# Casting the high halves of queries and keys on ScalarE instead of VectorE

## What is computed

```python
qkv = x_flat @ qkv_w.T + qkv_b
q, k, v = (qkv[0], qkv[1], qkv[2])
q = _l2norm(q)
k = _l2norm(k)
attn = jnp.einsum('bhnd,bhmd->bhnm', q, k) * temperature
attn = jax.nn.softmax(attn, axis=-1)
out = jnp.einsum('bhnm,bhmd->bhnd', attn, v)
```

## Time and profile before

| | us |
|---|---|
| median of 3 runs | 2742.59 (2740.02 to 2743.46) |
| the profiled execution | 2741.01 |
| its span, first to last instruction | 2739.1 |
| of that before the first exponential | 109.6 |
| attention, first to last exponential | 109.6 to 1652.0 |
| TensorE busy | 2465.8 (90%) |
| ScalarE busy | 1780.7 (65%) |
| VectorE busy | 1683.5 (61%) |
| GpSimd busy | 1420.5 (52%) |

### The profile page before, as it was taken

How to read it: one execution, slowest core, us unless ns; L and a number is a source line. 1 busy time by engine, 2 the same in 40 slices (tenths; PEclk the granted TensorE clock), 3 DMA queues, 4 the chain that set the end, 5 groups by cost and what they waited for, 6 DMA issues and landing times. The chain is left out here.

```text
span 2739.1 us, 58873 instructions
## 1 busy us (share of the span) xinstructions
PE 2465.8 (90%) x18693; PEld 1295.9 (47%) x18693; DVE 1683.5 (61%) x4886; ACT 1780.7 (65%) x2228; POOL 1420.5 (52%) x1137
## 2 busy tenths in 40 slices
PE   3699999999989999989999973999999999999975
PEld 2333333333333333333333321777777777777754
DVE  6557766866766766676676655555555555555522
ACT  2487777777778777767777852555565556555542
POOL 2334435534543543543454323677777777777750
PEclk9799999999999999999999987999999999999987
DMA  4221112112112111211211243444444444444429
GB/s 91 58 51 41 50 49 58 48 42 54 51 44 60 48 49 47 58 41 45 59 48 45 77 162 128 179 155 155 177 155 162 169 155 170 160 158 174 153 79 332
DMA packets 160322, 276.49 MB, mean 101 GB/s; under 512 B 21568, under 2 KB 129584, under 8 KB 150624
## 3 DMA queue, kind: packets, MB, share of 16 engines
q1 hardware_dynamic: 141648, 245.37, 27.8%
q0 software_dynamic: 13392, 27.97, 2.8%
q10 hardware_dynamic: 5056, 0.42, 0.3%
HBM read 174.07 MB, written 49.69 MB: 82 GB/s over the span
## 5 line engine op out<-in xcount | busy, mean ns | idle before, releaser
L788 ACT ACTIVATE probs<-ps_s 128x1024 f32<-128x1024 f32 x1024 | 1011.9, 1023 | 282.6 <-PE ps_s L687 260.0
L1360 POOL TENSOR_TENSOR h_split<-h_f,h_split 128x512 f16<-128x512 f32 x444 | 550.7, 1241 | 238.3 <-ACT h_f L1337 231.0
L1333 ACT ACTIVATE h_split<-ps_h,packs 128x512 f16<-128x512 f32 x444 | 305.2, 687 | 391.1 <-PE ps_h L1287 368.8
L1287 PE MATMUL ps_h<-m_xn_t,packs 128*128 128x512 f16 x2220 | 552.4, 380 | 0.5 <-DVE m_xn_t L1422 0.5
L700 PE MATMUL ps_o<-probs,v_aug 128*32 128x512 f32 x4096 | 550.6, 610 | 0.4 <-ACT probs L788 0.4
L1054 POOL TENSOR_TENSOR inv_norm<-sumsq,minus_half 128x16 f32<-128x16 f32 x128 | 378.0, 2953 | 312.4 <-DVE sumsq L997 307.6
L1301 PE MATMUL ps_y<-packs,h_split 128*128 128x192 f16 x5328 | 511.9, 245 | 0.9 <-POOL h_split L1360 0.9
L1301 PEld LDWEIGHTS ps_y<-packs,h_split 128*128 128x128 f16 x5328 | 453.0, 97 | 105.7 <-POOL h_split L1360 1.9
L687 PE MATMUL ps_s<-stacks_odd 98*128 98x512 f16 x1024 | 301.5, 386 | 17.0 <-DMA stacks_odd<-heads 10.2
L687 PE MATMUL ps_s<-even 98*128 98x512 f16 x1024 | 299.0, 383 | 11.6 <-ACT probs L788 5.7
L1337 ACT ACTIVATE h_f<-ps_h,packs 128x512 f32<-128x512 f32 x444 | 302.0, 680 | 0.0
(11 more groups left out here) (213 smaller groups left out, 2812.6 us busy)
## 6 DMA issues: line engine op xcount, KB each, us to landing
packs<-expert_pack SPq DMA_DIRECT2D x74, 1635.0 KB, 6.6
even<-heads SPq DMA_DIRECT2D x192, 96.0 KB, 2.4
stacks_odd<-heads SPq DMA_DIRECT2D x192, 96.0 KB, 2.4
tile_rows<-sorted_rows SPq DMA_DIRECT2D x37, 400.0 KB
tokens<-in_x_dram SPq DMA_DIRECT2D x17, 768.0 KB, 5.3
y_in<-y_tokens SPq DMA_DIRECT2D x16, 768.0 KB, 8.9
out_dram<-y_out SPq DMA_DIRECT2D x16, 768.0 KB, 7.1
even<-heads SPq DMA_DIRECT2D x128, 48.0 KB
```

What stands on the lines that cost most here:

```text
L788: act.activation(probs[:, u % PRING, :], ps_s[:, u % 2, :, :].rearrange("p f n -> p (f n)"), ACT.Exp).then_inc(s_probs, 1)
L1287: mm = pe.matmul(ps_h[:, n % HBUF, :], w1(par, slot, w, k), xn_t[0:rows_k, par, c, :], start=(i == 0), stop=(i == 4))
L1333: act.activation(h_split[:, n % HSPLIT, 0, :], ps_h[:, n % HBUF, :], ACT.Gelu, bias=bias1(par, slot, k), scale=1.0 / WSCALE)
L1360: pool.tensor_tensor(h_split[:, n % HSPLIT, 1, :], h_f32[:, n % HBUF, :], h_split[:, n % HSPLIT, 0, :], ALU.subtract).then_inc(s_h, 1)
```

## The change

ScalarE makes the high half of tile r-1, behind the exponential and the jobs of unit U+1 (`HIGH_AT = 1`). Two semaphores are new: `s_scaled` says that the scaling (L1007) has ended, and ScalarE waits for it; `s_high` says that the cast has ended, and VectorE waits for it ahead of the low half. VectorE's cast and its own wait behind it are gone. The low half stays in unit U+3.

```diff
+HIGH_AT = 1
-PRE_STEPS = 50 + NT
+PRE_STEPS = 50 - NT
...
+            if has_pre(img) and u - HIGH_AT in ROUNDS[1:NT + 1]:
+                high_heads(act, img, ROUNDS.index(u - HIGH_AT) - 1)
+
+    def high_heads(act, img, t):
+
+        act.wait_ge(s_scaled, NT * (img + 1) + t + 1)
+        if t >= QRING:
+            wait_taken(act, img, ("q", t - QRING))
+        elif not (isinstance(img, int) and img == -1):
+            act.wait_ge(s_job_act, jobs_before(img, True))
+        act.activation(qk_split[:, t % QRING, :, 0:HD], qk[:, t % QKRING, :, :], ACT.Copy).then_inc(s_high, 1)
...
-            pre.now(dve.tensor_tensor(qk[:, t % QKRING, :, :], scale16[:, :].unsqueeze(2).to_broadcast([P, 2 * NH, HD]),
-                                      qk[:, t % QKRING, :, :], ALU.mult))
-        elif part == 1:
-            if t >= QRING:
-                wait_taken(dve, img, ("q", t - QRING))
-            pre.now(dve.tensor_copy(high, qk[:, t % QKRING, :, :]))
+            dve.tensor_tensor(qk[:, t % QKRING, :, :], scale16[:, :].unsqueeze(2).to_broadcast([P, 2 * NH, HD]),
+                              qk[:, t % QKRING, :, :], ALU.mult).then_inc(s_scaled, 1)
+            dve.wait_ge(s_scaled, NT * (img + 1) + t + 1)
         else:
+            dve.wait_ge(s_high, NT * (img + 1) + t + 1)
             dve.tensor_tensor(low, qk[:, t % QKRING, :, :], high, ALU.subtract).then_inc(s_qk, 1)
...
-                if v in (0, 2, 3) and 0 < r <= NT:
-                    split_heads(dve, img, r - 1, pre, (0, 2, 3).index(v))
+                if v in (0, 3) and 0 < r <= NT:
+                    split_heads(dve, img, r - 1, pre, (0, 3).index(v))
```

More of the change, by code:

```diff
@@ L594, in attention_phase @@
     s_qk = sem("s_qk")
+    s_scaled = sem("s_scaled")
+    s_high = sem("s_high")
     s_rep_q, s_rep_k = ([sem(f"s_rep_{kind}{r}") for r in range(2)] for kind in "qk")
```

## The result

The changed kernel takes 2770.63 us as a median (2768.79 to 2771.19, 4 runs) against 2742.79 (2740.02 to 2743.46, 4 runs) for the kernel before beside it: a ratio of 1.0103, 95% interval 1.0091 to 1.0115. That is 27.8 us more, where +20 was predicted. The sign was right and 2770.6 lies inside the range, but about a third of the loss came from a place that the prediction didn't look at.

The account below looks back on a forecast made before the run. TensorE was taken to pace attention, so relief of VectorE gains nothing. Twelve loop images cost 14.9 us, images 1 and 2 2.4, image 0 3.7, less 0.5: 20.5 on 2741.0, about 2762 as a median, range 2739 to 2780.

Parts of the forecast that it names:

- What bounds the kernel: Attention phase: TensorE paces it; VectorE giving up 128 casts, 46 us of busy time, gains 0 there.
- ScalarE's step: Each cast lasts 512 ns on ScalarE and, as instructions overlap, delays what follows by about 0.42 us (bounds 0.39 and 0.51).
- Tiles 5, 6, 7 in the loop: Late exponentials delay TensorE's scores by 0.42, 0.06 and 0.76 us, the last by waiting for VectorE's scaling: 1.24 an image.
- Tiles 0 to 4 hidden: In an image of the loop, the casts of the first five tiles cost TensorE nothing.
- The sum: Whole kernel: 20.5 us added to the profiled 2741.0 gives 2761.5, about 2762 for a median, 0.7% slower.
- Image -1, "0.5 us gained": Before the first scores: only the last tile's cast is on the path, and moving it to ScalarE gains 0.5 us.
- Images 0 and 1: Image 0 loses 3.7 us: 0.42 each for tiles 1 to 6, 1.19 for tile 7; image 1 about 1.2.
- The rule weighed: VectorE's cast blocks GpSimd through a shared port; without it the power ends up to 0.36 earlier, 2758 us; left out.
- the waits of rows 2: TensorE's waits for VectorE's "v" eviction (L839): 33.5 us in 42 waits over 1544 us, forecast to stay near 33.
- full cost for every cast: Rival: no tile is hidden, 120 casts by 0.42 are 50 us, tile 7's wait adds 5: 2798; chance 0.08.
- the two with relief: Rivals: VectorE's relief offsets ScalarE's load, 2743, chance 0.16; or earlier "v" evictions gain 15 to 19 us, 2725, chance 0.12.
- What would show it: Signs: cast 0.49 to 0.53 us, ScalarE idle some 0.35 at tile 7, loop image 1.2 longer, expert phase unchanged.

Follow-up runs that it names:

- e8_five_pad20: Changed kernel with only tiles 0 to 4 cast on ScalarE, plus 20 unused VectorE writes so its loop starts at 740: 2733.44 us, ratio 0.9997.
- e12_last_three_pad12: Changed kernel with only tiles 5, 6, 7 cast on ScalarE, plus 12 unused VectorE writes (loop from 740): 2751.81 us, ratio 1.0079.
- e13_unit_two_pad32: Changed kernel with all eight casts one unit later, behind the jobs of unit U+2, plus 32 unused VectorE writes: 2747.50 us, ratio 1.0051.
- e4_first_five: Changed kernel with only tiles 0 to 4 cast on ScalarE, tiles 5 to 7 back on VectorE, no unused writes: 2750.52 us, ratio 1.0036.
- e3_no_cast: Kernel before without any cast: high halves zero, low half the whole number in f16, ScalarE as before: 2740.69 us, ratio 0.9995.

## Why the prediction was right, and where it fell short

- **What bounds the kernel**: right. TensorE paces it, and 46 us taken from VectorE bought nothing: 0.9995 (0.9984 to 1.0006) without any cast.
- **ScalarE's step**: 0.42 predicted, 0.41 measured; the cast 512 and 514 ns.
- **Tiles 5, 6, 7 in the loop**: 1.24 predicted, 1.16 measured where the code lies well, 1.17 as the mean of the change on the first chip, where the twelve bodies gave 14.1 against 14.9.
- **Tiles 0 to 4 hidden**: right in the loop (`e8_five_pad20`, `e12_last_three_pad12`). Wrong for image -1.
- **The sum**: 2761.5 for the profiled execution and 1.6 for the median give 2763, not "about 2762"; nothing hangs on it. That 2770.6 lies inside the range is luck in part. The prediction had no term for the returns; terms that were too large (image 0, the bodies) and the last image's 2.0 took back a part of what they cost.
- **Image -1, "0.5 us gained"**: half right. With only the last three tiles on ScalarE the first exponential comes at 108.81 instead of 109.44, 0.63 gained. In the change it comes 0.25 later, since the cast of tile 0 stands ahead of the third "n" eviction on ScalarE. That eviction was at 56.41 and is now at 58.94, behind the cast:

```profile
58.51 0.52 ACT L823 ACTIVATE heads<-heads 128x384 f16<-128x384 f32 x1 [4.85 <-DVE heads L1021]
58.94 0.47 ACT L802 ACTIVATE xn_t<-ps_m 128x384 f16<-128x384 f16 x1
```

  The step that failed is "image -1 has no exponentials ... the cast is no part of that": I asked what the cast delays, and not what stands behind its new wait. With the cast behind the "n" eviction (`e13_unit_two_pad32`) it is 108.73.
- **Images 0 and 1**: image 0 cost 2.8 instead of 3.7, image 1 3.5 instead of 1.2. At the end of image 0, TensorE waits 1.29 us for an exponential, and then works at the lower clock (0.50 from 189 to 191):

```profile
185.98 0.61 PE L690 MATMUL ps_s<-even 98*128 98x512 f16 x2 [1.29 <-ACT probs L791]
186.89 0.60 PE L690 MATMUL ps_s<-even 98*128 98x512 f16 x2 [0.31 <-ACT probs L791]
187.43 1.81 PE L703 MATMUL ps_o<-probs,v_aug 128*32 128x512 f32 x8
```

  The kernel before has no drop there. Over image 1 the other kernels with casts or copies at the last tiles lose between 1.4 and 3.9 us on either chip. Some 1.2 of it goes with the clock: the changed kernel on the second chip has no such fall, and image 1 takes 106.25 there instead of 107.43 (103.94 before). Of the 2.3 that are left, 1.2 was forecast; the rest stays open.
- **The missing term**: "the sum" knew only bodies. The step that failed is that the five jumps back to the loop's start were put at nothing, without a reason. VectorE's code became shorter by 32 instructions ahead of the loop and by 60 in it, and with that its restart became later, at least 4.47 us instead of 3.56, and TensorE waited up to 2.4 us for `tokens`. Five returns cost 9.9 us on the first chip, 7.6 on the second, the share of the clock in it included; small stalls of the same kind inside the iterations cost 0.6 an iteration there. On one chip the shift took back 10.6 us of the 33.7 that the change costs there (2766.64, 2755.99, 2732.98). That the cause is the place of VectorE's instructions is shown by the shifts. Which places are bad isn't: starts at 708 and 720 are, 740 and 772 aren't, and `e3_no_cast`, from 709 and with 122 transfers, isn't either. What the restart waits for stays open: more transfers of instructions go with the late restart of the change, but the times of single ones don't fit both late kernels.
- **The rule weighed**, of the Trainium skill (SBUF — State Buffer, "SBUF: two separate sides"): the trace spoke against it and the runs agree. Freed of the cast, the power takes 2917 ns for 2954 before, 0.04 shorter and not 0.36, and the waits of rows 2 grew from 33.5 to 38.4 instead of shrinking by 4. The 0.36 was too much in any case: the power starts while the cast already runs, and in most tiles overlaps it for 0.19.
- **The rivals**: full cost for every cast (2798) fell with `e4_first_five`; the two with relief fell with `e3_no_cast`.
- Of "What would show it": the waits for "v" should have stayed near 33 and grew by 4.9, which no sign of being wrong covered (it named only a shrinking by more than 5). They measure little. The larger row is the same (26.7 in 28) in `e4_first_five`, whose bodies are shorter than those of the kernel before. The other signs came as written.

## What to carry to other kernels

Between engines, work moves at the price of the exact places it goes to: eight equal casts cost 0, 0, 0, 0, 0, 0.41, 0.03 and 0.72 us, and following two chains (what the paced engine waits for next, what stands behind a new wait) gives these to a few hundredths. Before crediting or blaming an edit for a per cent, look at the loop's returns apart from its bodies, and at waits that no semaphore ended. If they changed, shift the code with a few unused instructions: if the time follows, a part of the difference is not the edit's.

## What was not expected of the hardware

- Taking 92 instructions from VectorE's program (32 ahead of the loop, 60 in it) made it restart later after a jump. 32 one-column writes that nobody reads gave 2766.64 us the value 2755.99, and 20 of them 1.0036 the value 0.9997.
- VectorE is back 3.6 us after its last instruction at the least, in all kernels here, from start to start, though the product that it needs can be ready at 2.5. TensorE, released by the DMA of `stacks_odd`, starts 0.2 to 1.1 us after `gx_res`.
- A wait of TensorE of 2.2 us or more can be paid again behind it, 1.94 for 1.06 us of product at 0.50 of the clock, but need not be: with waits of 2.3 to 3.0 us at its returns the kernel before had a fall at four of five in one profile and at one of five in the other.
- Two chips differ by 0.2% in this kernel (2739.7 and 2733), and the mean body by 0.6 of 88.9 us (one profile each).
